# A Mamba cross-attention and a ternary feed-forward on one core: one convolution a tile later, POOL's alpha series six steps later, projections and row groups ahead of sums

## The chip, the cores and the metric

The kernel runs on one core of one Trainium2 chip, in one launch. The metric is device microseconds of that core. A profiled execution gives the trace, whose times run from the first instruction to the last (its span); the execution's own time lies some 2 us above the span.

## What is computed

The reference takes x (4 x 512 x 512) and a context (4 x 512 x 256), all float32. Cut to what matters:

```python
def ssm(ctx, z):                      # per batch: 512 channels, 512 time steps, 16 states
    x  = in_proj_w @ ctx
    u  = silu(causal_depthwise_conv4(x) + conv_b)
    dt_lo, Bm, Cm = split(x_proj_w @ u)            # 16 + 16 + 16 rows
    delta = softplus(dt_proj_w @ dt_lo + dt_b)
    state = state * exp(delta * A) + (delta * u) * Bm    # a scan over time
    y = (state . Cm + D * u) * silu(z)
    return y.T

x = x + tanh(g_xattn) * ssm(ctx, layernorm(x))

def bit_linear(v, w, g):
    vq = round_to_127_levels(rmsnorm(v) * g)       # a scale per row
    wq = round(tanh(w / s)) * arctanh(s)           # s = mean |w|: ternary weights
    return vq @ wq.T

def ffn(v):
    return bit_linear(silu(bit_linear(v, w1, g1)) * bit_linear(v, w2, g2), w3, g3)

x = x + tanh(g_ffn) * ffn(layernorm(x))
```

## The kernel before

**Tiles and steps.** The state-space part works on 16 tiles k (KQ): tile k is 128 of the 512 channels (et = k % 4) of batch k // 4. A tile has four steps q, so there are 64 steps s = 4k + q. One step takes 32 channels times 16 states: the 128 partitions hold 32 channels times 4, and the remaining 4 states lie side by side in the free dimension, in two halves of two. In each step:

- SP copies delta of 32 channels into four groups of partitions (`bcast_delta`, line 501).
- ScalarE makes dA, four exponentials of 511 columns (`exps`, line 951, recorded as L962).
- TensorE replicates delta * u with a selection matrix into the bank `du_ps` (`bcast_du`, line 1649, L1657). There is one such bank: the broadcast for step s waits until VectorE has made both products of step s - 1.
- VectorE multiplies it with B (`add_input`, L1265, 1.23 us) and scans (`scan`, L1274, 2.29 us), for each half: the order is add_input(s, 0), scan(s, 0), add_input(s, 1), scan(s, 1), and the rest of its work stands in the gaps between them.
- POOL multiplies the states with C (`times_c`, L756, 4.5 us), one step behind.
- TensorE sums the states of two steps (`sum_states`, L1665, 16 matmuls) into `y_ps`.

Per tile there is also: the input projection of tile k + 5 (`in_proj`, L1619), the convolution as four diagonal matmuls (`convolve`, L1638, eight records) and its evacuation on ScalarE (`conv_evac`, L899), the skip term, the product with silu(z) on VectorE (`gated_y`, L1418), its transposition (`transpose_yz`, L1788) and the addition to x1 (`add_scan`, L1301). Every odd tile makes the step sizes of the next two (`sizes_due`): two projections (`dt_proj`, L1647), a table load, two softplus (L947), a table load. Once a batch, in tiles 3, 7 and 11, x_proj of the next batch (L1629, eight records) is evacuated by ScalarE (L931); x_dbl goes through a scratch in HBM and comes back replicated as B and C.

**Weights.** Twelve chunks of 1 MB (w1, w2, w3) are loaded, their absolute values summed on ScalarE (`abs_sum`, L1019, 1.9 us each), and the buffers filled again: SP requests chunk c + 3 as soon as chunk c is summed (`next_chunk`, L530). `abs_chunks(s)` gives the chunks summed in step s: chunk 3 in step 1, 4 and 5 in step 2, 6 in step 3, 7 and 8 in step 4, 9 in step 5, 10 and 11 in step 6. In step 7 (TERN_AT) VectorE adds the sums (L1386) and makes the scales (L1393 to L1399). From step 7 on POOL scales and rounds one chunk a step (`tern`, L785), TensorE transposes it (L1595) and ScalarE writes it as fp8 signs (L1134).

**alpha.** arctanh(s) comes from a series on POOL, `alpha_small` (line 788, L791 to L797): 18 operations on three columns, each waiting for the one before. Its constants lie in the buffer of g1, so SP loads g1 after it (semaphore `at_series`). VectorE then does `alpha_large` (line 1401) at step ALPHA_AT: a comparison (L1403), a multiply (L1406), a predicated copy (L1407), a product with the gate (L1409).

**Feed-forward.** Row ft is 128 of the 2048 rows. Its work runs in the same tiles, f = k - 4 and g = k - 5: in tile k row f is normalised, gained on POOL (`mul_gains`), quantised and transposed, and in step q = 3 its gate and up groups are computed (`gate_up`, L1712: for each of four chunks c four matmuls for gate and four for up), and evacuated by ScalarE (L972, L980). In tile k row g's hidden values are multiplied (`times_up`, L684) and gained (`h_gain`, L677) on POOL, their maxima taken on VectorE (L1435), quantised on ScalarE (L1035), transposed (L1769) and multiplied with w3 (`down`, L1814). `keep_clock` (L1777) puts in filler matmuls ahead of some waits. Rows 12 to 15 (TAIL = 12) come after the last tile, where VectorE multiplies the groups itself (`mul_up`, L1289).

**What sets the order.** Each engine runs its own list in the order written by hand. Nearly all TensorE results go through a ring of four banks of PSUM; `ring_order()` (line 84) lists the jobs in the order in which TensorE takes the banks, and a job waits for the evacuation of the job four before it (`freed_by`, line 334). When a convolution is made is set by two functions:

```python
def early_convs(k):
    if k < LEARLY or k % ET == ET - 1:      # LEARLY = 5, ET = 4
        return []
    m = k + AHEAD - (k % ET == 0)           # AHEAD = 5
    return [m] if m < KQ else []
```

So tile 5 makes convolution 10 and tile 6 convolution 11. Early convolutions stand ahead of the broadcast in step q = 1, late ones behind the skip term. In tile 5 the step sizes of tiles 6 and 7 are made as well. x_proj(b + 1) stands in step q = 0 behind `sum_states(2 * k - 1)` (line 1834). In the last step of the last tile TensorE does `sum_states(30)`, the groups 0 and 1 of row 11, `last_sums()`, `transpose_yz(15)`, groups 2 and 3.

## Time and profile before

| | us |
|---|---|
| median of 3 runs | 682.55 (681.11 to 682.89) |
| profiled execution, its own time | 679.72 |
| its span | 677.9 |
| TensorE matmuls busy | 598.8 (88%) |
| VectorE busy | 605.6 (89%) |
| ScalarE busy | 556.2 (82%) |
| POOL busy | 546.8 (81%) |
| mean granted clock of TensorE | 0.945 of full speed |
| chain that ended last, by engine | TensorE 44%, VectorE 34%, issue 8%, ScalarE 7%, POOL 6%, DMA 1% |

How to read it: busy is the sum of instruction times of one engine over the span, the rest is idle. The chain is followed back from the last instruction, at each step to what released it, so its shares say which engine the end waited for, on the average of all stages. Four engines are above 80% busy. Rows of the order of time have the start, the duration, the engine, the line, the operation, out<-in with shapes, how many instructions are merged in the row, and in brackets the idle time of the engine just before and what ended it.

### The profile page before, as it was taken

Reading aid. Unit: us, or ns where it says so; the run is one execution under the profiler, and the core shown is the slowest. Engines: PE = TensorE matmul, PEld = TensorE weight load, DVE = VectorE, ACT = ScalarE, POOL = GpSimd, SP = SyncE. Lnnn points to the kernel's source line nnn. Section 1 sums busy time; section 2 is a strip of 40 time slices with the busy share of each in tenths; the row PEclk is TensorE's granted clock in tenths of the full one; section 3 lists DMA queues with packets and bytes.
Section 4 is the critical chain, followed back from the end, with each engine's and each line's share of the span. In section 5 each row is a group of like instructions: output and inputs, shape, how many; then the busy total and the mean of one; then the engine's idle time right before and its main releaser. Section 6 shows DMA issues by size and latency. Waiting matters only on the chain.

```text
span 677.9 us, 8263 instructions
## 1 busy us (share of the span) xinstructions
PE 598.8 (88%) x2552; PEld 246.5 (36%) x2552; DVE 605.6 (89%) x582; ACT 556.2 (82%) x808; POOL 546.8 (81%) x340
## 2 busy tenths in 40 slices
PE   6987856989879999969999999978898989697997
PEld 3432212535343434323333433332433333233443
DVE  3999978989997899989899999989999999979675
ACT  3699892869799998988799998889889878847874
POOL 5146559877997999988899999998999999967840
PEclk9969767989899999989999999979897989899999
DMA  7799792739740213145121121144212121000000
GB/s 209 252 294 355 241 307 55 237 91 307 215 159 14 61 46 94 48 113 125 46 63 46 49 55 47 43 108 109 63 47 58 36 52 42 15 16 0 17 32 32
DMA packets 40573, 71.25 MB, mean 105 GB/s; under 512 B 10913, under 2 KB 13473, under 8 KB 38481
## 3 DMA queue, kind: packets, MB, share of 16 engines
q1 hardware_dynamic: 37312, 61.28, 31.8%
q10 hardware_dynamic: 3216, 9.44, 4.1%
q8 instruction: 21, 0.34, 0.2%
q14 instruction: 24, 0.19, 0.1%
HBM read 49.46 MB, written 4.46 MB: 80 GB/s over the span
## 4 chain that ended last, share of the span: by engine, by line
PE 44%; DVE 34%; issue 8%; ACT 7%; POOL 6%; DMA 1%; SPq 0%; DVEq 0%; ACTq 0%; POOLq 0%
DVE hb L1274 18%; PE ring L1712 10%; PE y_ps L1665 9%; DVE dbu_ps L1265 8%; PE ring L1814 5%; PE du_ps L1657 5%; PE ring L1638 4%; PE ring L1619 3%; POOL hb L756 3%; ACT dA L962 2%; PE ring L1777 2%; PE ring L1629 2%; DVE am L1330 1%; PE ring L1769 1%; PE ring L1595 1%
## 5 line engine op out<-in xcount | busy, mean ns | idle before, releaser
L1274 DVE TENSOR_TENSOR_SCAN hb<-dA,dbu_ps 128x1024 f32<-128x1024 f32 x128 | 292.2, 2283 | 8.6 <-PE y_ps L1665 1.7
L756 POOL TENSOR_TENSOR hb<-hb,bc_rep 128x2048 f32<-128x2048 f32 x52 | 235.9, 4536 | 28.6 <-DVE hb L1274 28.1
L1265 DVE TENSOR_TENSOR dbu_ps<-du_ps,bc_rep 128x1024 f32<-128x1024 f32 x128 | 157.8, 1232 | 16.8 <-PE du_ps L1657 9.4
L962 ACT ACTIVATE dA<-dl_rep,a_neg 128x511 f32<-128x511 f32 x256 | 163.4, 714 | 2.9 <-DMA dl_rep<-delta 2.3
L1665 PE MATMUL y_ps<-hb,sel_q 128*32 128x512 f32 x496 | 122.0, 637 | 3.9 <-POOL hb L756 3.7
L1657 PE MATMUL du_ps<-du,sel_q 32*128 32x512 f32 x128 | 74.5, 662 | 37.4 <-DVE dbu_ps L1265 37.2
L684 POOL TENSOR_TENSOR h<-h,up_sb 128x1024 f32<-128x1024 f32 x24 | 56.7, 2363 | 14.7 <-ACT up_sb L980 13.1
L1814 PE MATMUL ring<-w3T,hT 128*128 128x512 fp8e4 x256 | 62.4, 391 | 0.8 <-DVE hT L1282 0.4
L1665 PEld LDWEIGHTS y_ps<-hb,sel_q 128*32 128x32 f32 x496 | 27.7, 116 | 85.5 <-issue 78.7
L677 POOL TENSOR_TENSOR up_sb<-h,g3b 128x1024 f32<-128x1024 f32 x23 | 54.2, 2356 | 1.9
L751 POOL TENSOR_TENSOR hb<-hb,bc_rep 128x1024 f32<-128x1024 f32 x22 | 51.9, 2360 | 3.7 <-DVE hb L1274 2.5
L1712 PE MATMUL ring<-w2T,a12T 128*128 128x512 fp8e4 x208 | 53.4, 379 | 0.9 <-DVE hb L1289 0.9
L1712 PE MATMUL ring<-w1T,a12T 128*128 128x512 fp8e4 x208 | 53.5, 380 | 0.0
L1657 PEld LDWEIGHTS du_ps<-du,sel_q 32*128 32x128 f32 x128 | 19.5, 190 | 74.4 <-issue 73.5
L1638 PE MATMUL ring<-u,diag_w 128*128 128x512 f32 (+3 forms) x96 | 43.4, 597 | 0.0
L972 ACT ACTIVATE h<-ring,deq 128x512 f32<-128x512 f32 x48 | 32.9, 685 | 10.0 <-PE ring L1712 9.9
L1777 PE MATMUL ring<-w1T,a12T 128*128 128x512 fp8e4 x146 | 39.9, 413 | 0.0
L980 ACT ACTIVATE up_sb<-ring,deq 128x512 f32<-128x512 f32 x48 | 32.9, 686 | 7.0 <-PE ring L1712 6.7
L1814 PEld LDWEIGHTS ring<-w3T,hT 128*128 128x128 bf16 x256 | 24.2, 100 | 38.8 <-issue 12.5
L1079 ACT ACTIVATE hT<-ring 128x1024 bf16<-128x1024 f16 x27 | 26.6, 1019 | 12.4 <-PE ring L1769 11.8
L1435 DVE TENSOR_REDUCE h_max<-up_sb 128x1 f32<-128x1024 f32 x30 | 36.3, 1210 | 0.3
L1035 ACT ACTIVATE up_sb<-up_sb,h_sc 128x1024 f32<-128x1024 f32 x30 | 32.7, 1137 | 2.3 <-DVE h_sc L1462 2.3
(199 smaller groups left out, 961.2 us busy)
## 6 DMA issues: line engine op xcount, KB each, us to landing
dl_rep<-delta SPq DMA_DIRECT2D x256, 64.0 KB, 2.0
bc_rep<-bc_scratch SPq DMA_DIRECT2D x28, 256.0 KB, 5.2
h<-in_L_ffn_w_dram SPq DMA_DIRECT2D x5, 1024.0 KB, 7.7
x<-in_L_ffn_w_dram SPq DMA_DIRECT2D x5, 1024.0 KB, 8.3
up_sb<-in_L_ffn_w_dram SPq DMA_DIRECT2D x5, 1024.0 KB, 8.5
xt<-in_x_dram SPq DMA_DIRECT2D x16, 256.0 KB, 3.6
out_dram<-x SPq DMA_DIRECT2D x16, 256.0 KB, 2.0
h<-in_L_ffn_w_dram ACTq DMA_DIRECT2D x3, 1024.0 KB, 6.2
```

What stands on the lines that cost most here:

```text
L677: g.tensor_tensor(gained(ft)[:, half], hidden(ft)[:, half], g3b[:, half], ALU.mult).then_inc(h_mul, 1)
L684: g.tensor_tensor(h[:, half], h[:, half], up_sb[:, half], ALU.mult).then_inc(h_pool, 1)
L756: g.tensor_tensor(hb[:, s % 4, :, :], hb[:, s % 4, :, :], c_rep(s // 16), ALU.mult)\
L962: ins = a.activation(dA[:, s % 2, i, 1:L], dl[:, 1:L], ACT.Exp, scale=a_neg[:, s % 16, i:i + 1])
L1265: v.tensor_tensor(dbu_ps[:, :, :], du_ps[:, :].unsqueeze(1).to_broadcast([P, 2, L]), b_rep(b)[:, 2 * half:2 * half + 2, :], ALU.mult).then ...
L1274: v.tensor_tensor_scan(hb[:, s % 4, 2 * half:2 * half + 2, :].rearrange("p a l -> p (a l)"), dA[:, s % 2, 2 * half:2 * half + 2, :].rearra ...
L1638: ins = mm(dst[:, shift:L], diag_w[:, m % ET, DC - 1 - shift, :], u[:, m % UB, 0:L - shift], start=(shift == 0), stop=(shift == DC - 1))
L1657: mm(du_ps[:, :], sel_q[rows, :], du[rows, k % 2, :], start=True, stop=True).then_inc(du_bc, 1)
L1665: ins = mm(y_ps[32 * q:32 * q + 32, :], sel_q[:, 0:32], hb[:, s % 4, i, :], start=False, stop=(i == NH - 1))
L1712: ins = mm(dst[:, :], rows_T(ft)[:, m, t, :], w[:, t, 512 * c:512 * (c + 1)], start=(t == 0), stop=(t == ET - 1))
L1777: mm(dst[:, :], rows_T(ft)[:, t % 2, t // 2 % ET, :], w1T[:, t % ET, 0:512], start=True, stop=True)
L1814: ins = mm(dst[:, :], hT[:, t, :], w3T[:, t, :], start=(t == 0), stop=(t == H // P - 1))
```

## The change

- `ALPHA_AT` goes from 12 to 15, `alpha_small` on POOL from step 7 to step 13 (ahead of `z_affine(1)`), and the loads of g1 and g2 on SP from steps 9 and 10 to steps 14 and 15.
- `early_convs`: tile 5 makes no convolution, tile 6 makes 10 and 11.
- ScalarE, step 2: conv_evac(4), abs_sum(4), conv_evac(5), abs_sum(5) instead of both evacuations and then both sums. Step 5: abs_sum(9) ahead of conv_evac(6).
- TensorE: the broadcast for step 21 goes from the start of tile 5 to between the third and fourth chunk of row 0's gate_up. In tiles 7 and 11 x_proj stands ahead of the state sums (in tile 3 behind them, as before). In the last step of tile 15 the groups 0 and 1 of row 11 stand ahead of `sum_states(30)`.
- VectorE, row 12 after the tiles: the statistics of rows 14 and 15 go from ahead of mul_up(12, 1) to behind the quantisation scales of row 13.

```diff
-ALPHA_AT = 12
+ALPHA_AT = 15
@@ def early_convs(k):
-    if k < LEARLY or k % ET == ET - 1:
+    if k < LEARLY or k % ET == ET - 1 or k == LEARLY:
         return []
+    if k == LEARLY + 1:
+        return [k + AHEAD - 1, k + AHEAD]
@@ sync
-                    if s == TERN_AT + 2:
+                    if s == ALPHA_AT - 1:
                         sp.wait_ge(at_series, 1)
                         sp.dma_start(g1b[:, :], g1.partition_broadcast(P)).then_inc(ld_g, 16)
-                    if s == TERN_AT + 3:
+                    if s == ALPHA_AT:
                         sp.dma_start(g2b[:, :], g2.partition_broadcast(P)).then_inc(ld_g, 16)
@@ gpsimd
-                    if s == TERN_AT:
-                        alpha_small()
...
                     if s == 3 * Q + 1:
+                        alpha_small()
                         z_affine(1)
@@ scalar
-                    if q == (1 if k else 2):
+                    if q == 1 and k > 1:
+                        for m in late_convs(k):
+                            conv_evac(m)
+                    if s == 2:
+                        conv_evac(ET)
+                        abs_sum(4)
+                        conv_evac(AHEAD)
+                        abs_sum(5)
+                    if s == Q + 1:
+                        abs_sum(9)
                         for m in late_convs(k):
                             conv_evac(m)
...
-                    for c in abs_chunks(s):
-                        abs_sum(c)
+                    if s not in (2, Q + 1):
+                        for c in abs_chunks(s):
+                            abs_sum(c)
@@ vector
-                if ft == TAIL:
-                    for late in (TAIL + 2, TAIL + 3):
-                        rows(late)
-                else:
+                if ft > TAIL:
                     mul_up(ft, 0)
                 mul_up(ft, 1)
                 if ft + 1 < NT:
                     quant_scales(ft + 1)
                     dequant_scales(ft + 1)
+                if ft == TAIL:
+                    for late in (TAIL + 2, TAIL + 3):
+                        rows(late)
@@ tensor
-                        bcast_du(s + 1)
+                        if f != 1:
+                            bcast_du(s + 1)
...
+                        if k > ET and et == ET - 1 and b + 1 < B:
+                            x_proj(b + 1)
                         if k >= 1:
                             sum_states(2 * k - 1)
-                        if et == ET - 1 and b + 1 < B:
-                            x_proj(b + 1)
+                        if k == ET - 1:
+                            x_proj(1)
...
-                        if f >= 0:
+                        if k == KQ - 1:
+                            gate_up(f, 0)
+                            gate_up(f, 1)
                             sum_states(2 * k)
-                            if f and s + 1 < Q * KQ:
+                            last_sums()
+                            transpose_yz(KQ - 1)
+                            gate_up(f, 2)
+                            gate_up(f, 3)
+                        elif f >= 0:
+                            sum_states(2 * k)
+                            if f:
                                 bcast_du(s + 1)
                             gate_up(f, 0)
-                        if f >= 0:
                             for c in range(1, 4):
-                                if k == KQ - 1 and c == 2:
-                                    last_sums()
-                                    transpose_yz(KQ - 1)
+                                if f == 0 and c == 3:
+                                    bcast_du(s + 2)
                                 gate_up(f, c)
```

## Rows read from the trace of the kernel before

**Rows 1.** Windows; columns: us, busy PE, PEld, DVE, ACT, POOL, clock, DMA share, GB/s

```profile
188.00:210.00 22.00, 17.46 (x102) 9.36 (x101) 19.59 (x15) 21.66 (x36) 18.94 (x9) 1.00 0.40 126
...
240.00:275.00 35.00, 35.00 (x157) 14.14 (x156) 33.94 (x29) 31.04 (x49) 33.35 (x20) 1.00 0.25 68
```

**Rows 2.** Order of time, ScalarE, steps 2 and 5: waits for a convolution

```profile
55.39 0.69 ACT L899 ACTIVATE u<-ring,convb_col 128x512 f32<-128x512 f32 x1 [1.63 <-PE ring L1638]
...
83.70 0.69 ACT L899 ACTIVATE u<-ring,convb_col 128x512 f32<-128x512 f32 x1 [1.87 <-PE ring L1638]
```

**Rows 3.** Order of time, VectorE, steps 7 and 9

```profile
92.54 0.17 DVE L1386 TENSOR_REDUCE at<-wsum 128x3 f32<-128x12 f32 x1 [3.55 <-ACT up_sb L1019]
...
114.29 0.69 DVE L1418 TENSOR_TENSOR yz<-y_ps,xt 128x512 f32<-128x512 f32 x1 [1.77 <-PE y_ps L1665]
```

**Rows 4.** Order of time, POOL and TensorE, steps 7 to 9

```profile
98.66 0.20 POOL L791 TENSOR_TENSOR at<-wm 128x3 f32<-128x3 f32 x1
...
103.47 4.50 POOL L756 TENSOR_TENSOR hb<-hb,bc_rep 128x2048 f32<-128x2048 f32 x1
...
108.02 6.22 PE L1665 MATMUL y_ps<-hb,sel_q 128*32 128x512 f32 x16 [2.04 <-POOL hb L756]
```

**Rows 5.** Order of time, VectorE and POOL, steps 12 to 14

```profile
138.28 1.97 POOL L785 TENSOR_SCALAR up_sb<-up_sb,w_inv 128x2048 f32<-128x2048 f32 x1
...
138.63 1.65 DVE L1403 TENSOR_SCALAR at_mask<-wm 128x3 uint32<-128x3 f32 x1
140.31 0.17 DVE L1406 TENSOR_SCALAR at<-at 128x3 f32<-128x3 f32 x1
...
152.67 1.23 DVE L1265 TENSOR_TENSOR dbu_ps<-du_ps,bc_rep 128x1024 f32<-128x1024 f32 x1 [1.74 <-PE du_ps L1657]
...
156.40 1.27 POOL L654 TENSOR_TENSOR du<-delta,u 128x512 f32<-128x512 f32 x1 [4.25 <-ACT delta L947]
```

**Rows 6.** Order of time, VectorE and POOL, at the start and at step 15

```profile
8.52 4.16 DVE L1233 TENSOR_SCALAR diag_d<-ident,d_col 128x128 f32<-128x128 f32 x4 [8.52 <-DMA d_col<-in_L_xattn_D_dram]
8.56 4.03 POOL L761 TENSOR_TENSOR diag_w<-ident,conv_col 128x512 f32<-128x512 f32 x4 [1.35 <-DMA d_col<-in_L_xattn_D_dram]
...
164.20 4.56 POOL L756 TENSOR_TENSOR hb<-hb,bc_rep 128x2048 f32<-128x2048 f32 x1
...
166.12 2.29 DVE L1274 TENSOR_TENSOR_SCAN hb<-dA,dbu_ps 128x1024 f32<-128x1024 f32 x1
...
168.74 1.97 POOL L785 TENSOR_SCALAR up_sb<-up_sb,w_inv 128x2048 f32<-128x2048 f32 x1
```

**Rows 7.** Order of time, TensorE, VectorE and ScalarE, tile 4

```profile
175.24 5.04 PE L1665 MATMUL y_ps<-hb,sel_q 128*32 128x512 f32 x16 [0.55 <-POOL hb L756]
...
183.86 0.75 DVE L1301 SCALAR_TENSOR_TENSOR x<-ring,gates,x 128x512 f32<-128x512 f32 x1 [0.20 <-PE ring L1788]
...
187.05 0.81 ACT L990 ACTIVATE a<-x,fsc 128x512 f32<-128x512 f32 x1 [1.22 <-DVE fsc L1322]
```

**Rows 8.** Order of time, TensorE and VectorE, tile 5: convolution 10 and the broadcast behind it

```profile
220.17 3.69 PE L1638 MATMUL ring<-u,diag_w 128*128 128x512 f32 x8
...
224.95 1.23 DVE L1265 TENSOR_TENSOR dbu_ps<-du_ps,bc_rep 128x1024 f32<-128x1024 f32 x1 [0.66 <-PE du_ps L1657]
```

**Rows 9.** Order of time, TensorE and VectorE, tile 6: broadcast and product of step 26

```profile
257.41 1.12 PE L1657 MATMUL du_ps<-du,sel_q 32*128 32x512 f32 x2
...
259.85 1.23 DVE L1265 TENSOR_TENSOR dbu_ps<-du_ps,bc_rep 128x1024 f32<-128x1024 f32 x1
```

**Rows 10.** Order of time, ScalarE, tiles 7 and 11: evacuation of x_proj

```profile
292.39 0.59 ACT L931 ACTIVATE xdbl<-ring 48x512 f32<-48x512 f32 x1 [2.96 <-PE ring L1629]
...
436.62 0.59 ACT L931 ACTIVATE xdbl<-ring 48x512 f32<-48x512 f32 x1 [1.26 <-PE ring L1629]
```

**Rows 11.** Order of time, ScalarE and VectorE, end of tile 15

```profile
596.02 1.03 ACT L1042 ACTIVATE a12T<-ring 128x1024 bf16<-128x1024 f16 x1 [3.17 <-PE ring L1796]
...
606.72 0.69 DVE L1418 TENSOR_TENSOR yz<-y_ps,xt 128x512 f32<-128x512 f32 x1 [3.85 <-PE y_ps L1676]
```

## The prediction, on record before the changed kernel was built

> **What bounds the kernel now.** I read the windows first, then each engine's order of time around each edit. No engine bounds the whole. From 188 to 210 us ScalarE is busy 21.66 of 22 us, from 240 to 275 TensorE 35.00 of 35 [rows 1]. Elsewhere VectorE, with two scans and two products per step, runs from one short wait to the next. A gain or a loss counts only where the chain passes at that moment, so each edit is priced at its own place. A step s is a quarter of a tile k. All times below are those of the kernel before. Its profiled execution took 679.72 us (span 677.9); the median of the runs shown is 682.55, 2.83 above it. I add my sum to the profiled time and carry it to the median unchanged. A measurement of this kernel can tell about 0.3%, some 2.0 us, from no change.
>
> **Weight sums on ScalarE (steps 2 and 5).** ScalarE waited 1.63 and 1.87 us for a convolution and then summed chunks [rows 2]. In the new order a sum of 1.9 us fills each wait. The first gain does not last: the softplus of step 5 waits for its projection. The second does, since VectorE idled 3.55 us for the last chunk sum and POOL's first ternary step hangs on it [rows 3]. Chunk 9 was requested long before it is used. **-1.87** (bounds -3.5 and 0).
>
> **alpha_small from step 7 to 13 on POOL.** Its 18 small operations ran from 98.66 to 103.47, and then came the C product of step 7; TensorE had idled 2.04 us for that, and VectorE 1.77 us for TensorE's sums [rows 3, 4]. Without them that product starts with its scan, over 4 us sooner, and TensorE is next held by the du broadcast behind VectorE's own product, so VectorE's wait goes whole: **-1.77**. At step 13 POOL idles 4.25 us for delta before 156.40 [rows 5]; the C product of step 12 starts 2.0 us sooner as well (next part), so 4.8 us fit into 6.3: 0. If that cover were gone, 4.8 us of POOL would lie on the chain. The two gain DMAs move to steps 14 and 15 of SP's queue, 0.6 us of issue each, behind at_series (ready by then) and ahead of load_c; the C product they could make late is not due before its scan, which is late itself (below): 0, up to +1.
>
> **alpha_large from step 12 to 15 on VectorE.** This is the largest term. At step 12 it took 2.2 us from 138.63 on, three quarters of it the first comparison. TensorE's broadcast for step 13 had been released before it, so its removal only lengthens VectorE's wait of 1.74 us at 152.67 [rows 5]: 0. At step 15 it stands ahead of the second scan, which started at 166.12. Two groups show what that costs. At step 12 the comparison on three columns took 1.65 us and ended with a POOL instruction that had begun just before it (138.28 + 1.97 = 140.25), where the next operation on three columns took 0.17 [rows 5]. At the start four VectorE operations on 128 columns took 1.04 us each, in step with four POOL products of 1.01 [rows 6]. So a VectorE operation of this kind waits for the POOL instruction under way, and behind it for another if POOL has one ready. At 165.95 POOL is inside the C product of step 14 (to 168.74), and the ternary step follows at once (to 170.7) [rows 6]. I take both holds: the comparison ends at 168.8, the multiply at 170.8, and the rest is free, because POOL's next product waits for the very scan that is held. The scan starts at 171.3 instead of 166.1, +5.2.
> The shown pairing for three columns is with a POOL TENSOR_SCALAR only. The Trainium skill, "SBUF — State Buffer", section "Who interferes with whom", says that VectorE in a two-port mode and GpSimd exclude each other for a whole instruction, whatever the GpSimd operation is. By that rule the first hold stands, and the sum is as I give it; if only the shown pairing counted, it would be one hold and 2.5 us less. No row here pairs three columns with the large product.
> Who waits: TensorE's broadcast for step 17 stands ahead of the sums of 175.24, so those come 4.5 us later; add_scan at 183.86 had 0.20 us of slack; ScalarE had idled 1.22 us for VectorE before the normalise of 187.05 and is full from there on [rows 1, 7]. **+4.9** (bounds: no hold, 0.7 us of operations less 0.2 of slack, +0.5; each of three operations held, +7).
>
> **Convolution 10 out of tile 5, broadcast 21 inside gate_up.** The convolution takes 3.69 us, and VectorE waited 0.66 us behind it [rows 8]. The broadcast in the middle of row 0's gate_up does not help: VectorE's next operation, the maximum, waits for POOL's gain either way. It pushes the last pair of groups, their evacuations and the exponentials behind them by 1.05 us, which takes back the 0.6. **0** (-0.7 to +1).
>
> **Two convolutions in tile 6, x_proj(2) ahead of the sums in tile 7.** In tile 6 TensorE has no gap [rows 1], and the broadcast for step 26 ends 1.3 us before VectorE wants it [rows 9]. 3.6 us more in front of it make VectorE 2.2 us late and everything behind it on TensorE 3.6. In tile 7 ScalarE idled 2.96 us for x_proj [rows 10]; moved ahead of 3.6 us of sums it takes back what TensorE lost on that path, all but 0.7, while gated_y, which needs these sums, is later. The hidden row reaches POOL late as well. I take **+1.0**; the ends are -1.6 (the convolution hidden; of ScalarE's 2.96 us, 1.3 are lost again at gated_y, whose sums come 3.6 us later) and +3.7 (nothing given back).
>
> **x_proj(3) in tile 11.** ScalarE's wait of 1.26 us for it goes [rows 10]; the sums, 3.6 us later, are ready when gated_y is due. The softplus, the normalise and TensorE's broadcast inherit it. **-1.26** (-1.3 to 0). x_proj(1) keeps its place.
>
> **Row 11's groups ahead of the last sums.** Before, the sums of step 61 ran while ScalarE evacuated the row's transposes (596.02 to 597.05), then four groups, then the last sums; VectorE idled 3.85 us for them [rows 11]. Now the groups wait for that evacuation: TensorE idles 1.1 us at 596, and the same three blocks of matmuls follow back to back. gated_y of the last tile comes **+1.05** later. The row's earlier evacuation ends on POOL, which then waits for VectorE's statistics of row 12 anyway, and those come after gated_y. Bounds: 0 to +1.5.
>
> **rows(14), rows(15) behind the quantisation of row 13.** The same operations stand ahead of mul_up(12, 2), whose bank TensorE awaits, so it keeps its time. POOL's first gain product of row 12 starts later, behind two powers that wait for these rows (two statistics, 2.0 us of VectorE); the maximum that needs it is followed by a wait of VectorE for TensorE's product anyway. **0** (-0.5 to +0.6).
>
> **Sum:** -1.87 - 1.77 + 4.9 + 0 + 1.0 - 1.26 + 1.05 = +2.05: 681.8 on the profiled execution, 684.6 on the median.
>
> **Rivals.**
> 1. One hold. The multiply gets in between POOL's two instructions, for it is issued some 0.05 us after the comparison. The hold is 2.8 us, the cost 2.5: sum -0.35, 682.2. For it: I infer who wins only from the operations of 128 columns. Chance 0.20.
> 2. No hold; the end is faster. Place: the comparison at step 15. Price: 0.5 instead of 4.9, sum -2.35, 680.2. It decides if POOL is not busy there, that is if its delta of tile 4 comes over 2 us sooner against VectorE than now, or if the large product leaves three columns alone. Against: POOL has had a backlog since delta came at 156.40, the product of step 13 and a ternary step stand ahead of the one of step 14 [rows 5, 6]. Chance 0.13.
> 3. The second convolution is covered in tile 6 (filler matmuls stand there while ScalarE quantises): -1.6 instead of +1.0, sum -0.55, 682.0. Against: filler is work that TensorE runs through. Chance 0.15.
> 4. TensorE bounds tiles 6 and 7 whole, +3.7 instead of +1.0: sum +4.75, 687.3. For it: gated_y of tile 6 waits for sums that now come 7 us later. Chance 0.12.
> 5. The reordering does nothing (all waits replaced one for one): 682.5. It shares its time with 1 and 3, which hold its chance.
>
> **How the numbers follow.** The forecast has 0.40, its own range is 682.8 to 686.8. 684.6 is the edge of 0.3%, so about half of it counts as slower, with all of rival 4 and a part of the mixtures: slower 0.41. Rival 2, and rivals 1 and 3 together (680 or less), give faster 0.22. Same 0.37. The range takes in rival 2's lower bound and most of rival 4: 679.5 to 688.0.
>
> **What the profile after would show.** VectorE's idle ahead of the weight sums down from 3.55 to about 1.7; no wait at the gated product of tile 1; a comparison at step 15 of about 2.8 us and a multiply of about 1.9, the second scan of step 15 over 5 us behind its product. A wait of VectorE of about 2.2 us for the du broadcast at step 26, and one at gated_y of tile 6. No wait of ScalarE at its copy of x_dbl in tile 11. At the end, TensorE idle 1.1 us ahead of row 11's groups and VectorE's last large wait near 4.9 us. The prediction is wrong if the comparison takes 0.2 us, or if tile 6 is not longer than before.

## The result and the profile after

**687.12 us** (5 executions, 685.84 to 688.88), against 682.82 for the kernel before on the same chip (681.11 to 682.89). The ratio is 1.0081, 95% interval 1.0057 to 1.0106: slower. The forecast was 684.6 (+2.05). In medians the difference is 4.3 us, by the ratio of the executions 5.5. The side was right, the size was not: more than half of the loss was not in the sum.

The profiled execution took 686.7 us (span 684.8, mean granted clock 0.937; before 679.72, 677.9, 0.945). Busy times on its page: TensorE 604.3 us, VectorE 609.1, ScalarE 556.2, POOL 547.3. TensorE has 5.5 us more than before for the same number of matmuls (2552 on both pages): a lower clock, not more work (598.8 x 0.945 and 604.3 x 0.937 give the same 566).

I compare profiled executions by VectorE's scans. The first one starts between 33.5 and 36.5 us in the kernels shown here (33.6 before), with the same instructions ahead of it; so its start is made common, and each later scan gives a delay against the kernel before. "s18" is the first scan of step 18, "s15.1" the second of step 15. Negative is sooner. The delays of a kernel are those of its one profiled execution. Ten kernels have the same code up to step 9 (the whole change, those that take something out of it later, and c_best), and they stand between -2.62 and -3.56 at s9.1: differences under 1 us between two kernels say little by themselves.

| stretch | forecast | after |
|---|---|---|
| to s14: weight sums, alpha_small | -3.64 | -3.59 |
| to s15.1: alpha_large | +5.2 | +5.00 |
| to s20: slack behind the hold, gains | -0.3 | +0.74 |
| to s25: tile 5 | 0 | +0.95 |
| to s34: tiles 6 to 8 | +1.0 | +2.34 |
| to s49: tile 11 | -1.26 | -2.08 |
| to s61.1 | 0 | +0.12 |
| to the end: last step | +1.05 | +1.71 |
| sum | +2.05 | +5.19 |

Now the rows. VectorE ahead of the weight scales, at the gated product of tile 1, at step 13 and around alpha_large, in order of time (start, us, then the engine; in brackets the idle time and what ended it):

```profile
91.72 0.17 DVE L1397 TENSOR_REDUCE at<-wsum 128x3 f32<-128x12 f32 x1 [1.66 <-ACT up_sb L1020]
...
112.44 0.69 DVE L1429 TENSOR_TENSOR yz<-y_ps,xt 128x512 f32<-128x512 f32 x1
...
150.79 1.23 DVE L1276 TENSOR_TENSOR dbu_ps<-du_ps,bc_rep 128x1024 f32<-128x1024 f32 x1 [3.72 <-PE du_ps L1668]
...
164.05 2.87 DVE L1414 TENSOR_SCALAR at_mask<-wm 128x3 uint32<-128x3 f32 x1
166.95 1.92 DVE L1417 TENSOR_SCALAR at<-at 128x3 f32<-128x3 f32 x1
168.91 0.17 DVE L1418 COPY_PREDICATED alpha<-at_mask,at 128x3 f32<-128x3 uint32 x1
...
169.24 2.28 DVE L1285 TENSOR_TENSOR_SCAN hb<-dA,dbu_ps 128x1024 f32<-128x1024 f32 x1
```

The wait of 3.55 us is 1.66, that of 1.77 us is gone [rows 3]. The wait of step 13 grew from 1.74 to 3.72 us [rows 5]: the idle time that alpha_large had filled. Comparison and multiply took 2.87 and 1.92 us, where 2.8 and 1.9 were forecast. POOL beside them, and its next two products:

```profile
162.33 4.56 POOL L758 TENSOR_TENSOR hb<-hb,bc_rep 128x2048 f32<-128x2048 f32 x1
166.88 1.97 POOL L787 TENSOR_SCALAR up_sb<-up_sb,w_inv 128x2048 f32<-128x2048 f32 x1
171.60 4.52 POOL L758 TENSOR_TENSOR hb<-hb,bc_rep 128x2048 f32<-128x2048 f32 x1 [2.75 <-DVE hb L1285]
...
179.43 4.52 POOL L758 TENSOR_TENSOR hb<-hb,bc_rep 128x2048 f32<-128x2048 f32 x1 [1.36 <-DMA bc_rep<-bc_scratch]
```

164.05 + 2.87 = 166.92 is the end of the product, 166.95 + 1.92 = 168.87 that of the ternary step. Both holds are there. The Trainium skill, "SBUF — State Buffer", section "Who interferes with whom" (a two-port VectorE operation and GpSimd exclude each other for a whole instruction, whichever began) is borne out for the TENSOR_TENSOR as well, at 2.87 us. That the comparison runs in such a mode no run shows. The last row has the wait for C, 1.36 us where 0.45 stood before. Yet this product starts only 0.13 us later against the first scan than before (144.12 for 143.99), and POOL later waits 2.54 us for VectorE (at 189.68), so the wait for C costs nothing here. The +0.74 up to s20 comes from TensorE (first row) and VectorE's waits for it (the other two):

```profile
176.71 2.04 PE L1668 MATMUL du_ps<-du,sel_q 32*128 32x512 f32 x2 [7.52 <-DVE dbu_ps L1276]
184.19 0.69 DVE L1429 TENSOR_TENSOR yz<-y_ps,xt 128x512 f32<-128x512 f32 x1 [0.21 <-PE y_ps L1676]
187.72 0.75 DVE L1312 SCALAR_TENSOR_TENSOR x<-ring,gates,x 128x512 f32<-128x512 f32 x1 [0.64 <-PE ring L1799]
```

TensorE idles 7.52 us for the held VectorE, its broadcast then takes 2.04 us instead of 1.09 (granted clock 0.50 from 175 to 180 us), and VectorE waits 0.21 and 0.64 us for it, where it waited 0 and 0.20: 0.65 of the 0.74. a_fill below has the same hold and no wait for C at all, and the same +0.76.

TensorE and VectorE in tile 6, order of time:

```profile
259.57 7.11 PE L1649 MATMUL ring<-u,diag_w 128*128 128x512 f32 x16
266.61 1.12 PE L1668 MATMUL du_ps<-du,sel_q 32*128 32x512 f32 x2
...
267.77 1.23 DVE L1276 TENSOR_TENSOR dbu_ps<-du_ps,bc_rep 128x1024 f32<-128x1024 f32 x1 [2.31 <-PE du_ps L1668]
...
301.65 0.69 DVE L1429 TENSOR_TENSOR yz<-y_ps,xt 128x512 f32<-128x512 f32 x1 [1.21 <-PE y_ps L1676]
```

The broadcast for step 26 stands behind both convolutions, and VectorE waits 2.31 us for it (2.2 forecast), then 1.21 us for the sums at gated_y of tile 6 (1.3 forecast as a bound). The last step of tile 15, TensorE and VectorE:

```profile
595.25 1.09 PE L1668 MATMUL du_ps<-du,sel_q 32*128 32x512 f32 x2 [0.70 <-DVE dbu_ps L1276]
596.27 2.76 PE L1825 MATMUL ring<-w3T,hT 128*128 128x512 fp8e4 x12
...
600.60 1.04 PE L1723 MATMUL ring<-w1T,a12T 128*128 128x512 fp8e4 x4 [1.12 <-ACT a12T L1043]
...
604.69 1.02 PE L1723 MATMUL ring<-w1T,a12T 128*128 128x512 fp8e4 x4 [2.19 <-DVE x L1438]
605.55 1.80 PE L1723 MATMUL ring<-w2T,a12T 128*128 128x512 fp8e4 x4
...
613.60 0.69 DVE L1429 TENSOR_TENSOR yz<-y_ps,xt 128x512 f32<-128x512 f32 x1 [5.54 <-PE y_ps L1687]
```

The wait of 1.12 us is the one forecast. The 2.19 us one is not: group pair 1 needs a bank of the ring that VectorE's output (L1438, 603.80 to 604.54) frees. Behind it TensorE falls to half clock (four matmuls in 1.80 us instead of 1.03), and the gated product waits 5.54 us instead of 3.85 [rows 11].

### The profile page after: what moved, and what is told of

Its sections match the earlier page's. It is cut to its first block, busy times and chain, and to the rows that moved or that the text cites. A ratio compares the mean times of both kernels' runs of the same rounds, so it can differ in the third digit from the quotient of the medians.

```text
span 684.8 us, 8263 instructions
## 1 busy us (share of the span) xinstructions
PE 604.3 (88%) x2552; PEld 246.9 (36%) x2552; DVE 609.1 (89%) x582; ACT 556.2 (81%) x808; POOL 547.3 (80%) x340
## 4 chain that ended last, share of the span: by engine, by line
PE 38%; DVE 35%; ACT 12%; issue 9%; POOL 4%; DMA 1%; SPq 0%; DVEq 0%; ACTq 0%; POOLq 0%
DVE hb L1285 18%; PE y_ps L1676 8%; PE ring L1723 8%; DVE dbu_ps L1276 8%; PE du_ps L1668 4%; PE ring L1825 4%; PE ring L1649 4%; ACT dA L963 3%; PE ring L1630 2%; POOL h L686 2%; PE ring L1788 2%; DVE am L1341 1%; PE ring L1780 1%; DVE hT L1229 1%; DVE h_max L1446 1%
## 5 line engine op out<-in xcount | busy, mean ns | idle before, releaser
L1668 PE MATMUL du_ps<-du,sel_q 32*128 32x512 f32 x128 | 77.9, 690 | 38.8 <-DVE dbu_ps L1276 38.8
L1723 PE MATMUL ring<-w1T,a12T 128*128 128x512 fp8e4 x208 | 53.5, 380 | 3.4 <-DVE x L1438 2.2
L1788 PE MATMUL ring<-w1T,a12T 128*128 128x512 fp8e4 x146 | 41.7, 427 | 0.0
L1630 PE MATMUL ring<-ctxT,w_inT 128*128 128x512 f32 x64 | 34.0, 668 | 0.7 <-ACT ctxT L871 0.7
```

Source lines behind the costliest of these rows:

```text
L1668: mm(du_ps[:, :], sel_q[rows, :], du[rows, k % 2, :], start=True, stop=True).then_inc(du_bc, 1)
L1723: ins = mm(dst[:, :], rows_T(ft)[:, m, t, :], w[:, t, 512 * c:512 * (c + 1)], start=(t == 0), stop=(t == ET - 1))
L1788: mm(dst[:, :], rows_T(ft)[:, t % 2, t // 2 % ET, :], w1T[:, t % ET, 0:512], start=True, stop=True)
```

## The experiments

Sixteen kernels, timed against the kernel before (its median is 681.3 to 681.6 beside them). First the edits one by one on the kernel before, and parts of the change taken out of the whole; then what these left open. Delays are against the kernel before, as in the table above.

| kernel | us | ratio (95%) | s15.1 | s18 | s25 | s34 | s49 | s61.1 | end |
|---|---|---|---|---|---|---|---|---|---|
| after | 687.12 | 1.0081 (1.0057-1.0106) | 1.41 | 2.15 | 3.10 | 5.44 | 3.36 | 3.48 | 5.19 |
| b_alpha | 685.13 | 1.0052 (1.0032-1.0071) | 1.53 | 2.55 | 2.55 | 2.89 | 3.06 | 3.08 | 3.13 |
| b_conv | 685.28 | 1.0042 (1.0026-1.0059) | 0.26 | 0.56 | -0.24 | 3.48 | 3.61 | 3.62 | 3.63 |
| b_xproj | 675.72 | 0.9894 (0.9871-0.9918) | -0.44 | 0.00 | 2.41 | -0.52 | -2.87 | -2.17 | -3.83 |
| b_tail | 682.04 | 1.0005 (0.9982-1.0029) | -0.66 | -0.22 | 2.18 | 2.42 | 2.54 | 2.52 | 2.56 |
| a_slot | 684.06 | 1.0030 (1.0005-1.0055) | -3.19 | 0.89 | 0.67 | 2.38 | 0.24 | 0.35 | 2.08 |
| a_cols | 684.20 | 1.0043 (1.0022-1.0063) | -0.46 | 0.76 | 1.14 | 2.63 | 0.39 | 0.97 | 2.70 |
| a_conv5 | 680.74 | 0.9985 (0.9963-1.0007) | 1.92 | 2.67 | 3.07 | 0.36 | -2.24 | -1.64 | -1.57 |
| a_fill | 685.30 | 1.0057 (1.0037-1.0077) | 2.16 | 2.92 | 2.73 | 5.32 | 3.69 | 3.69 | 3.76 |
| c_gains | 682.87 | 1.0017 (1.0000-1.0034) | -3.23 | -1.90 | -1.89 | -0.63 | -2.99 | -2.27 | -0.51 |
| c_convx | 678.92 | 0.9968 (0.9949-0.9987) | -0.46 | -0.47 | -1.03 | -0.34 | -2.78 | -2.04 | -3.70 |
| c_absx | 674.72 | 0.9902 (0.9881-0.9922) | -2.67 | -1.31 | -1.07 | -3.69 | -5.88 | -5.34 | -6.95 |
| c_best | 674.01 | 0.9891 (0.9875-0.9907) | -3.42 | -2.10 | -1.90 | -4.55 | -6.76 | -6.18 | -7.81 |
| d_xtail | 677.71 | 0.9951 (0.9928-0.9973) | 0.28 | 0.33 | 0.33 | -2.78 | -5.26 | -4.52 | -2.77 |
| d_notail | 683.93 | 1.0032 (1.0014-1.0050) | 2.36 | 3.13 | 4.07 | 6.44 | 4.36 | 4.47 | 2.83 |
| d_nobc | 685.31 | 1.0052 (1.0035-1.0068) | 0.04 | 2.92 | 2.10 | 2.96 | 0.62 | 1.38 | 3.12 |
| d_noxp | 692.70 | 1.0160 (1.0133-1.0188) | 2.15 | 2.91 | 3.85 | 9.21 | 8.05 | 8.74 | 10.46 |

**b_alpha: the alpha edits alone.**

```diff
-ALPHA_AT = 12
+ALPHA_AT = 15
-                    if s == TERN_AT:
-                        alpha_small()
...
                     if s == 3 * Q + 1:
+                        alpha_small()
```

> The kernel before with the alpha edits alone (alpha_small to step 13, alpha_large to step 15, g1 and g2 loads to steps 14 and 15). Theory: the wait of 1.77 us at tile 1's gated product goes, alpha_large costs 5.0 us at step 15 and 0.7 more by tile 5: +3.5 to +4.0 us against before, 686.3 to 686.8. Rival (the two parts cancel, the loss of the whole change is elsewhere): within 1.5 us of before.

Measured +0.52%, 3.5 us. The trace has the two holds again (s15.0 to s15.1: -3.73 to +1.53). The terms -1.77 and +4.9 give +3.1, which is near, but the parts are not those of the sum. At s9.1 the kernel stands at -2.03, as forecast. Another 1.6 us come in step 12, from which alpha_large is gone (forecast: 0), and stay, for the sums of that step take 3.63 us; in the whole change they take 5.30, as before (5.32), and the 2.0 us that step 12 brings are gone at s14. Behind the hold 1.0 us is lost by s18, again VectorE's waits for TensorE (0.48 and 0.64 us).

**b_conv: the convolutions alone** (the edit of early_convs and nothing else).

> The kernel before with the convolution edit alone (none in tile 5, two in tile 6), x_proj where it was. Theory: 1.5 to 2 us lost in tile 5 by TensorE's half clock behind the idle time, then TensorE 3.6 us late through tile 6, and x_proj(2) gives nothing back: +4 to +5.5 us, 686.8 to 688.3. Rival (my forecast's pricing of tile 5 at 0, tile 6 by VectorE's wait of 2.2 us): +2.2 us, 685.

Measured +0.42%, in medians 3.6 us, all of it between s25 and s34: between theory and rival. The loss in tile 5 that the theory had does not show; from s20 to s25 the kernel gains 0.53 us.

**b_xproj: x_proj ahead of the sums, in tiles 7 and 11, alone.**

```diff
+                        if k > ET and et == ET - 1 and b + 1 < B:
+                            x_proj(b + 1)
                         if k >= 1:
                             sum_states(2 * k - 1)
-                        if et == ET - 1 and b + 1 < B:
-                            x_proj(b + 1)
+                        if k == ET - 1:
+                            x_proj(1)
```

> The kernel before with x_proj(2) and x_proj(3) ahead of the state sums. Theory: 2.05 us faster in tile 11, as in the changed kernel (5.1 against 7.15 us of delay), and 1.6 to 2 us in tile 7: 3 to 4 us faster than before, 679 to 680. Rival (my forecast for tile 11, 1.26 us, and gated_y's sums coming late in tile 7): 1.5 to 2.8 us faster.

Measured -1.06%, in medians 5.9 us: the best single edit. The trace has -2.93 from s25 to s34, -2.35 from s34 to s49, and -1.66 behind s61.1, where nothing was edited. It is above both expectations; the last part is not the edit's own work but the place where the clock falls (see d_notail).

**b_tail: row 11's groups ahead of the last but one sums, alone.**

```diff
+                        if k == KQ - 1:
+                            gate_up(f, 0)
+                            gate_up(f, 1)
+                            sum_states(2 * k)
+                            last_sums()
```

> The kernel before with row 11's groups 0 and 1 ahead of the sums of step 61 alone. Theory: TensorE idles for the evacuation of the row's transposes, gated_y of tile 15 comes 1.1 to 1.7 us later and the end with it: +1.1 to +1.7 us, 683.9 to 684.5. Rival (the earlier groups give it back behind the last tile): within 0.5 us of before.

Measured +0.05%: nothing. The forecast of +1.05 took the same blocks of matmuls to follow one another. The gated product waits 3.89 us, as long as before, though TensorE has two waits, 1.12 and 0.50:

```profile
593.92 1.09 PE L1657 MATMUL du_ps<-du,sel_q 32*128 32x512 f32 x2 [2.32 <-DVE dbu_ps L1265]
594.95 4.45 PE L1814 MATMUL ring<-w3T,hT 128*128 128x512 fp8e4 x12
...
600.96 1.04 PE L1712 MATMUL ring<-w1T,a12T 128*128 128x512 fp8e4 x4 [1.12 <-ACT a12T L1042]
...
603.36 1.02 PE L1712 MATMUL ring<-w1T,a12T 128*128 128x512 fp8e4 x4 [0.50 <-DVE x L1427]
...
610.62 0.69 DVE L1418 TENSOR_TENSOR yz<-y_ps,xt 128x512 f32<-128x512 f32 x1 [3.89 <-PE y_ps L1676]
```

What pays for them is below, at d_notail.

**a_slot: the whole change, alpha_large behind the second scan of step 13.**

```diff
-                    if s == ALPHA_AT:
-                        alpha_large()
                     scan(s, 1)
+                    if s == 3 * Q + 1:
+                        alpha_large()
```

> The changed kernel with alpha_large alone moved, from ahead of the second scan of step 15 to behind the second scan of step 13, where VectorE waits 3.7 us for a du broadcast. Theory (POOL's instructions hold the two operations on three columns, 4.8 us, and everything behind inherits it): the second scan of step 15 starts 5 us sooner against the first scan of step 14, and nearly all of it stays to the end: 5.0 to 5.7 us faster than the changed kernel, so 681.5 to 682.5, within 0.3% of before. Rival (POOL's backlog of tile 4 is the bound and the held scan costs little behind it): the scan starts sooner but tile 5 does not, at most 2 us faster than the changed kernel.

The hold is gone (s15.1 at -3.19 instead of +1.41), yet only 3.1 us of 4.6 stay (684.06, between theory and rival): from s15.1 to s18 it loses 4.08 us. 1.4 of it are VectorE's waits for TensorE (0.78 and 0.64 us), 2.8 a wait for POOL, which waits for C. POOL, VectorE, then SP's queue:

```profile
181.44 4.54 POOL L758 TENSOR_TENSOR hb<-hb,bc_rep 128x2048 f32<-128x2048 f32 x1 [5.71 <-DMA bc_rep<-bc_scratch]
...
189.71 0.21 DVE L1333 TENSOR_SCALAR fsc<-fmv,fsc 128x1 f32<-128x1 f32 x1 [2.76 <-POOL fsc L716]
```

```profile
157.39 0.58 SPq L584 DMA_DIRECT2D g1b<-in_L_ffn_g_dram  x1
...
165.64 0.58 SPq L586 DMA_DIRECT2D g2b<-in_L_ffn_g_dram  x1
166.27 2.51 SPq L499 DMA_DIRECT2D bc_rep<-bc_scratch  x4
```

The loads of the gains, moved with alpha, now stand ahead of the load of C for batch 1: that of g2 directly, that of g1 some 9 us earlier.

**a_cols: comparison and multiply of alpha_large one column at a time,** still in step 15.

```diff
-                link(v.tensor_scalar(at_mask[:, :], wm[:, :], 0.25, None, ALU.is_ge))
+                for c in range(3):
+                    ins = v.tensor_scalar(at_mask[:, c:c + 1], wm[:, c:c + 1], 0.25, None, ALU.is_ge)
```

> The changed kernel with the comparison and the multiply of alpha_large made one column at a time, three operations each, at the same place in step 15. Theory (only an operation of more than one column takes what POOL holds, as the one-column operations beside POOL's products show no hold): each takes 0.15 to 0.2 us, the whole of alpha_large about 0.9 us instead of 5.2; 4 us faster than the changed kernel, about 683. Rival (POOL's large product holds every VectorE operation that goes from SBUF to SBUF): the first column's comparison takes about 2.8 us, no gain.

```profile
162.92 4.55 POOL L758 TENSOR_TENSOR hb<-hb,bc_rep 128x2048 f32<-128x2048 f32 x1
...
164.63 0.26 DVE L1415 TENSOR_SCALAR at_mask<-wm 128x1 uint32<-128x1 f32 x3
164.93 0.28 DVE L1422 TENSOR_SCALAR at<-at 128x1 f32<-128x1 f32 x3
165.24 2.25 DVE L1426 COPY_PREDICATED alpha<-at_mask,at 128x3 f32<-128x3 uint32 x1
```

Six operations of one column ran in 0.54 us inside POOL's product; the same work on three columns was held for 4.8. The predicated copy, left at three columns, then took the hold (2.25 us, to the end of POOL's product), so one of two holds went: s15.1 at -0.46, and 2.9 us less than the whole change, not 4 (the intervals overlap).

**a_conv5: the whole change with convolution 10 back in tile 5.**

> The changed kernel with convolution 10 back in tile 5. Theory (without the convolution TensorE idles 2.9 us in tile 5, its clock drops and it does the transposes' filler and the first products of w3 at half speed; in tile 6 the second convolution then delays VectorE by 2.3 us): the filler ahead of the w3 products takes 1.03 us again instead of 1.91, the wait of 2.31 us at step 26 goes; 3 to 5 us faster than the changed kernel, 682 to 684. Rival (tile 5 gains from the missing convolution, as ScalarE's list is shorter): tile 5 gets 0.5 to 1 us longer, tile 6 2.3 us shorter, net 1.5 to 2 us faster than the changed kernel.

680.74: 6.4 us under the whole change, more than the theory's 3 to 5, where the convolutions alone cost 3.6. The waits of step 26 go (s25 to s34 is -2.71 instead of +2.34). Another 1.6 us are in the last step, whose code is that of the whole change:

```profile
600.02 1.02 PE L1721 MATMUL ring<-w1T,a12T 128*128 128x512 fp8e4 x4 [2.19 <-DVE x L1436]
600.88 1.03 PE L1721 MATMUL ring<-w2T,a12T 128*128 128x512 fp8e4 x4
...
607.29 0.69 DVE L1427 TENSOR_TENSOR yz<-y_ps,xt 128x512 f32<-128x512 f32 x1 [3.89 <-PE y_ps L1685]
```

The same wait of 2.19 us, and no half clock behind it.

**a_fill: the whole change with 22 instead of 10 filler matmuls in tile 5,** where the convolution had been.

> The changed kernel with 22 instead of 10 filler matmuls ahead of the hidden transposes of row 0 in tile 5, 2.6 us of work in the idle time that the convolution left. Clock theory: the filler and the four products behind the transposes take 1.03 us each again instead of 1.91 and 1.76, row 1's gate_up starts 1.5 to 1.9 us sooner against the first scan of tile 5, and 1 to 1.9 us of it stays to the end (685 to 686). Rival (the loss in tile 5 is the order of the transposes behind ScalarE's quantiser): the durations come back but gate_up does not come sooner, no gain.

685.3, 1.8 us under the whole change, with overlapping intervals. In its trace s20 to s25 is -0.18 instead of +0.95: TensorE idles 0.34 us instead of 2.93 ahead of the transposes and no longer falls to half clock behind them (1.03 + 1.03 us for 1.91 + 1.76). Counted from s20, 0.9 us of that is left at s34 and 0.5 at s61.1. The rest of its lead at the end (3.76 for 5.19) is the last step, which loses 0.07 instead of 1.71 without the half clock, as in a_conv5, with the code of the whole change. So the filler's own gain is 0.5 to 1.1 us by the trace. s25 to s34 stays (+2.59): the main cost of the convolutions is in tile 6.

What was open now: C's landing, whether conv and x_proj add, and whether the weight sums gain at all.

**c_gains: a_slot with both gains loaded in step 16, behind C.**

```diff
-                    if s == ALPHA_AT - 1:
+                    if s == ALPHA_AT + 1:
                         sp.wait_ge(at_series, 1)
...
-                    if s == ALPHA_AT:
+                    if s == ALPHA_AT + 1:
                         sp.dma_start(g2b
```

> a_slot with the loads of g1 and g2 issued in step 16, behind the load of C of batch 1 and delta of step 18, instead of in steps 14 and 15 ahead of it. In a_slot the C product of step 16 waited 5.71 us for C (181.44), against 0.45 us in the kernel before (177.59). Theory: DMA is full there (share 1.00 from 160 to 180 us), the two gains are 0.5 MB in the same queue ahead of C, so C lands about 2 us later for them. Then POOL's wait falls from 5.7 to 2 to 4 us, the scan of step 18 comes 1.5 to 3 us sooner against the kernel before, and the time is 681 to 683 (684.1 for a_slot). Rival: C lands when the weight chunks in the other queue let it, wherever the gains stand: the wait stays above 5 us and the time within 0.7 us of a_slot's.

POOL's product in this kernel:

```profile
177.10 4.53 POOL L758 TENSOR_TENSOR hb<-hb,bc_rep 128x2048 f32<-128x2048 f32 x1 [1.44 <-DMA bc_rep<-bc_scratch]
```

177.10 for 181.44, s18 at -1.90 for +0.89: the theory, and more than the 2 us by which I had explained it. Timed it is 1.2 us, and the two intervals overlap, so this verdict rests on the traces. They agree: from the issue of C's load to the product that waited for it, 11.1 to 13.0 us pass in the five kernels with the gains loaded early (before, b_conv, b_xproj, b_tail, c_absx), 13.8 to 17.0 in the eight with them ahead of C, and 11.5 and 11.0 in c_gains and c_best. The DMA engines are full there: in the windows of the kernel before their share is 1.03, 1.07 and 1.00 in the three stretches of 5 us from 160 on and falls to 0.65 in the fourth; in a_slot it is 0.96 even in the fourth. (The expectation has 1.00 up to 180 us, which holds, nearly, for a_slot only.) The 0.5 MB of the gains would take 1.5 to 2.3 us at the 229 to 355 GB/s of those windows of a_slot (an estimate); why C lands still later is open.

**c_convx: convolutions and x_proj together.**

> The kernel before with two edits: early_convs (tile 6 makes convolutions 10 and 11) and x_proj ahead of the sums in tiles 7 and 11. Alone they cost 3.6 us and gained 5.9 us. Theory: the second convolution in tile 6 uses up TensorE's room in tiles 6 to 8 that the moved x_proj gains from, so that the two together are worse than their sum: 681 to 683, and the convolutions cost 5.3 to 7 us beside the moved x_proj. Rival: the two effects add: 679.4, and the larger cost of the convolutions inside the whole change (6.4 us) comes from tile 5, where the whole change also has its broadcast inside gate_up.

678.92: the rival. The two effects add (3.6 - 5.9 = -2.3; measured -2.7). The theory that x_proj's gain needs the room that the convolution takes is out.

**c_absx: x_proj and the weight sums.**

> The kernel before with x_proj ahead of the sums in tiles 7 and 11 and ScalarE's weight sums in the new order (steps 2 and 5). x_proj alone took 675.7 us. Theory: the weight sums gain about 2 us at VectorE's first scan of step 7, as in the whole change, but they are swallowed by step 12: the whole change, with the alpha edits and the weight sums, stood at -3.59 us at the first scan of step 15, the alpha edits alone at -3.73. So within 0.7 us of 675.7. Rival, my forecast: the gain of 1.87 us stays, 673.8.

674.72, in medians 1.0 us under x_proj alone, between both; by the ratios (0.9902 and 0.9894) it is no faster, so the timing can't tell the gain of the sums from nothing. At s9.1 they are worth 2.2 us (-2.61 against -0.44 in c_convx), at s18 0.8 (-1.31 against -0.47). Between the two VectorE waits 0.82 and 0.64 us for TensorE, whose broadcast takes 1.63 instead of 1.09 us and whose sums take 6.38 instead of 5.05: an earlier VectorE finds TensorE at the lower clock there. It has no wait for POOL, so this loss is not the landing of C.

**c_best: everything that gained** (x_proj, the weight sums, alpha_small at step 13, alpha_large behind the scan of step 13, the gains behind C; convolutions, broadcast and last step as before).

> Everything that gained: x_proj ahead of the sums in tiles 7 and 11, the weight sums, alpha_small at step 13, alpha_large behind the second scan of step 13, the gains loaded behind C. Convolutions, broadcast and the last step as before. x_proj alone took 675.7 us; the scan of step 15 comes 3.3 us sooner. Theory: 0 to 3 us of it are kept past the C product of step 16, 673 to 676. Rival: C's landing swallows all, and the cover for alpha_small is thin: 676 to 678.

**674.01**, ratio 0.9891 (0.9875 to 0.9907), in the range of the theory: it beats both kernels, by 1.1% and by 1.9%. Against c_absx the alpha edits bring 0.7 us, which these executions can't tell from nothing.

The single edits sum to +0.6 us in medians (3.5 + 3.6 - 5.9 - 1.0 + 0.4) and to 0.0 by the ratios; the whole is +4.3 in medians, 5.5 by the ratio. The broadcast and rows(14), rows(15) were not put alone. The last four kernels look for what the edits do to each other.

**d_xtail: x_proj and the last step. d_notail: the whole change, the last step as before.**

> The kernel before with two edits: x_proj ahead of the sums in tiles 7 and 11, and row 11's groups ahead of the last but one sums. Alone they took 675.7 and 682.0 us, against 681.6. Theory: in the last step group pair 1 needs a ring bank that VectorE's output frees. Where x_proj is moved, TensorE waits 2.19 us for it (a_conv5, after) instead of 0.50 (row 11's groups alone), and with the 1.12 us ahead of pair 0 the gain of 1.66 us that x_proj has behind step 61 is lost: 677.3 to 679.3, and more where the clock falls behind that wait. Rival: the edit of the last step costs nothing here either: 675.5 to 676.3.

> The whole change with the last step of tile 15 in its old order. From the scan of step 61 to the end the whole change loses 1.7 us against the kernel before; the kernels with x_proj moved and the old last step gain 1.65 there. Theory: 3.4 us are the two waits of the new order (1.12 and 2.19 us) with the clock drop behind them: 683.2 to 684.5. Rival: the clock drop at the end has other causes, and only the forecast's 1.05 us come back: about 686.

677.71 and 683.93, as both theories have it: the new order of the last step costs 2.0 us beside x_proj and 3.2 us in the whole change, where alone it had cost nothing. The gated product's wait, VectorE's order of time: 3.85 us before, 3.89 in b_tail, 2.16 in b_xproj and in d_notail, 5.53 in d_xtail, 5.54 after, and 3.89 in a_conv5 and a_fill. TensorE in d_xtail:

```profile
586.54 2.76 PE L1814 MATMUL ring<-w3T,hT 128*128 128x512 fp8e4 x12
...
594.96 1.87 PE L1712 MATMUL ring<-w1T,a12T 128*128 128x512 fp8e4 x4 [2.19 <-DVE x L1427]
596.61 1.87 PE L1712 MATMUL ring<-w2T,a12T 128*128 128x512 fp8e4 x4
598.41 2.34 PE L1665 MATMUL y_ps<-hb,sel_q 128*32 128x512 f32 x10
...
601.48 2.34 PE L1676 MATMUL y_ps<-hb,sel_q 128*32 128x512 f32 x10
```

and in d_notail:

```profile
601.37 3.63 PE L1676 MATMUL y_ps<-hb,sel_q 128*32 128x512 f32 x16
...
608.48 3.65 PE L1687 MATMUL y_ps<-hb,sel_q 128*32 128x512 f32 x16
```

Three facts make these values. (1) In the kernel before and in b_tail the twelve w3 matmuls of that step take 4.45 us, in b_xproj, d_xtail, d_notail and after 2.76: a half-clock stretch falls elsewhere, and TensorE is 1.69 us earlier (3.85 to 2.16). It is not x_proj itself that does this: d_noxp below has x_proj in its old place and 2.76 us too. (2) With the new order TensorE can't use that: VectorE's output frees the bank of group 1, and it starts 8.56 us behind the broadcast for step 63 before and 8.55 after, and takes 0.74. So TensorE's wait for it grows from 0.50 to 2.19. (3) The two blocks of sums, 3.63 + 3.65 = 7.28 us apart, take 598.41 to 603.82, 5.41 us, back to back: they write different 32 partitions of y_ps, and their records interleave. These 1.87 us pay for 1.12 + 0.50 in b_tail.

With TensorE early the bill is 1.12 + 2.19 - 1.87 = 1.4 us, where 1.7 are measured (2.16 to 3.89, a_conv5 and a_fill). In the whole change and six others (d_xtail, a_slot, a_cols, c_gains, d_nobc, d_noxp) the clock also falls behind the wait of 2.19 us: two blocks of four take 1.87 us each instead of 1.03 in d_xtail, and the wait goes on to 5.53. These further 1.6 us are not bound to the wait alone, for a_conv5 and a_fill have it without them; why the clock falls in seven and not in two is open.

**d_nobc: the whole change, broadcast 21 at the start of tile 5.**

> The whole change with the broadcast for step 21 back at the start of tile 5. From step 20 to step 25 the whole change lost 0.95 us and the kernel with the convolutions and x_proj alone, whose broadcast is in the old place, gained 0.56. Theory: the broadcast inside gate_up costs 1.0 to 1.5 us: 685.6 to 686.2. Rival, my forecast: nothing, as in the two kernels without the hold of step 15, which lose 0 there: within 0.5 us of 687.1.

685.31, 1.8 us less than the whole change, as the theory has it, though the intervals overlap. TensorE in tile 5, of the whole change and then of this kernel:

```profile
232.23 0.62 PE L1780 MATMUL ring<-ident,up_sb 128*128 128x128 f16 x8 [2.93 <-ACT up_sb L1036]
...
233.83 1.91 PE L1788 MATMUL ring<-w1T,a12T 128*128 128x512 fp8e4 x4
235.53 1.76 PE L1825 MATMUL ring<-w3T,hT 128*128 128x512 fp8e4 x4
```

```profile
231.91 0.62 PE L1780 MATMUL ring<-ident,up_sb 128*128 128x128 f16 x8 [2.62 <-ACT up_sb L1036]
...
233.41 1.03 PE L1788 MATMUL ring<-w1T,a12T 128*128 128x512 fp8e4 x4
234.28 1.03 PE L1825 MATMUL ring<-w3T,hT 128*128 128x512 fp8e4 x4
```

With the broadcast late in tile 4 the transposes start 23.47 us behind the first scan of step 20 instead of 22.31, TensorE idles 2.93 instead of 2.62 us ahead of them, and behind that the clock falls to its lower level in the whole change (1.91 + 1.76 for 1.03 + 1.03, 1.6 us) and not in this kernel. It is no fixed price. From s20 to s25 three kernels with convolution 10 gone and the broadcast in the old place gain 0.5 us (b_conv, c_convx, this one); with the broadcast in the new place four gain 0.2 (a_slot, a_cols, c_gains, a_fill) and three lose 0.95 (after, d_notail, d_noxp). In a_slot the half clock falls on the ten fillers (4.06 us instead of 2.32), in time that TensorE would have idled.

The broadcast also has a price in tile 6: from s25 to s26 the three with two convolutions and the old place lose 2.4 us, the seven with the new place 2.8 or 3.4.

This kernel also shows rival 1 by chance, in step 15. POOL's ternary step waited for its chunk, and the multiply got in ahead of it:

```profile
164.82 2.85 DVE L1414 TENSOR_SCALAR at_mask<-wm 128x3 uint32<-128x3 f32 x1
167.71 0.17 DVE L1417 TENSOR_SCALAR at<-at 128x3 f32<-128x3 f32 x1
...
168.99 1.98 POOL L787 TENSOR_SCALAR up_sb<-up_sb,w_inv 128x2048 f32<-128x2048 f32 x1 [1.34 <-DMA up_sb<-in_L_ffn_w_dram]
...
183.63 4.54 POOL L758 TENSOR_TENSOR hb<-hb,bc_rep 128x2048 f32<-128x2048 f32 x1 [6.23 <-DMA bc_rep<-bc_scratch]
```

One hold instead of two put s15.1 at +0.04. By s18 it was +2.92 all the same: VectorE waited 1.09 and 0.64 us for TensorE and 1.25 for POOL, whose product had waited 6.23 us for C.

**d_noxp: the whole change, x_proj behind the sums.**

> The whole change with x_proj behind the sums everywhere, as before. Alone x_proj gained 5.9 us, 1.66 of it behind step 61, where the whole change has none of it. Theory: inside the whole change it is worth 2.5 to 4 us, so 689.6 to 691. Rival: the gain is whole, 692.5 to 693.5.

692.7: the rival. x_proj is worth 5.6 us inside the whole change, as it is alone. In the trace 3.9 us of it lie between s25 and s49 (+4.20 here, +0.26 in the whole change), 0.6 behind; the remaining 0.75 stands at s25 already, ahead of the first edited instruction, and is no effect of it (the kernels with the same code there differ by 0.9 us at s9.1). Here the intervals are clear of each other (1.0057 to 1.0106, 1.0133 to 1.0188).

## Why the forecast was right or wrong

The forecast failed in its size. Four stretches of the table hold the miss: behind the hold (+1.0), tile 5 (+0.95), tiles 6 to 8 (+1.3) and the last step (+0.7 in the table, 2.3 in truth, see below). In three of them (not in tiles 6 to 8, as far as shown) TensorE's lower clock behind a wait has a part, and the sum had no term for it. Rival 4 has nearly the measured number, 687.3, but by luck: it put the whole of the miss, +2.7, into tiles 6 and 7, where the trace has half of it.

**Weight sums -1.87, alpha_small -1.77: right** at s9.1, in mechanism and size: -2.17 and -2.03 alone, -3.56 together. That the sum also fits at s14 (-3.64 against -3.59) hangs on step 12. Taking alpha_large from there was priced at 0; it brings 2.0 us at s13 that are lost again at s14, as forecast, but in b_alpha, whose sums of that step run at full clock, 1.7 stay. Later the gain of the sums melts to what timing can't show (c_absx).

**alpha_large +4.9: right in its mechanism**, its two holds and their sizes (+5.0 at s15.1). Rival 1 is what d_nobc's trace has: it hangs on when a chunk's DMA lands. What neither I nor the rivals had is that the hold covers C's landing: without the hold a_slot waits for C instead.

**"The two gain DMAs move to steps 14 and 15 … 0, up to +1": within its bounds in the whole change, wrong in its reason.** I priced their issue on SP's queue. But the DMA engines are full there, and C does land later. The hold and POOL's slack cover that (0.13 us later at the product, nothing behind it); where the hold is gone it is 2.8 us by the trace (a_slot to c_gains).

**The slack behind the hold, -0.3: the first failed step.** Between s15.1 and s20 I only had 0.20 us of slack at add_scan. The trace has +0.74: TensorE idles 7.52 us for the held VectorE and comes back at half clock.

**Broadcast 21, convolution 10 out of tile 5: 0: mis-sized**, near the edge of its bound (-0.7 to +1): +0.95 in the trace. The 0.66 us of the convolution's wait were nearly all won (0.5 in three kernels). The broadcast inside gate_up costs 0.3 to 1.5 us in tile 5 and 0.4 to 1.0 at step 26; timed it is 1.8 (d_nobc, overlapping intervals). I looked for who waits, and not for what the clock does with the hole, nor for what a late TensorE means in tile 6.

**Two convolutions in tile 6, x_proj(2) +1.0: right in mechanism** (2.31 us at step 26, 1.21 at gated_y), and nearly in size without the broadcast's edit: c_convx has +0.69 there, d_nobc +0.86, the whole change +2.34. So 1.5 of the 1.65 us between c_convx and the whole change go with the broadcast: 1.0 at step 26, where TensorE comes in late with no slack left; the rest is not settled. That a_conv5 gains 6.4 us and not 3.6 is for 1.6 us the half clock of the last step (0.07 behind s61.1 instead of 1.71) and for 1.3 in tiles 6 to 8, where the late TensorE costs only with the second convolution.

**x_proj(3) -1.26: too small.** ScalarE's wait is gone as forecast, but s34 to s49 gives -2.08 (-2.35 alone). In the kernel before VectorE waited 0.83 us for POOL (447.09) and 1.22 for the broadcast (452.18) in tile 11; both waits are gone.

**Row 11's groups +1.05: the second failed step, and the largest single error.** "The same three blocks of matmuls follow back to back" was wrong twice: the sums overlap (-1.87), and a second wait was missed, that of group 1 for VectorE's output. I had followed the new order's first operand (a12T) and not the bank that its second needs. By itself the edit costs 0, in the whole change 3.2 us (d_notail; intervals 1.0014 to 1.0050 and 1.0057 to 1.0106): 1.7 by its order once TensorE is early, and 1.6 by the half clock behind the new wait. The table hides most of it, because a half-clock stretch of 1.7 us left this step for a place outside it, which was luck. That it costs nothing alone and 3.2 us here is why neither the forecast's sum nor a test of each edit by itself finds it.

**rows(14), rows(15): 0: right**, as far as the traces tell: d_notail, which has this edit and the old last step, gains 1.64 us behind s61.1, the four kernels with neither edit 1.61 to 1.66.

Of the whole, x_proj gains 5.6 us; the hold (3.1), the last step (3.2), the broadcast (1.8) and the convolutions (3.6 or more) take it back twice over. Each is the difference of two medians, good to about 1 us, and the parts overlap, so they are not to be added up to the last tenth.
